# Packs of K and Q by 6 transfers instead of 12, and a first stage that loads only what the first products need

## The reference

```python
# cross-attention, 16 heads of width 16
q = (layernorm(x) @ Wq.T + bq); k = (ctx @ Wk.T + bk); v = (ctx @ Wv.T + bv)
x = x + softmax(q k^T / 4) v @ Wo.T + bo
# feed-forward block: h0 = layernorm(x)
h = h0 + causal_attention_with_rope(rmsnorm(h0, g1), wq, wk, wv) @ wo
y = h + moe(rmsnorm(h, g2), w_router, wg, wu, wd)      # 8 experts, top 2, hidden 704
x = x + y
```

## Time and profile before

| | |
|---|---|
| median of 3 runs | 2783.26 us (2781.7 to 2789.47) |
| the profiled execution's own time | 2782.65 us |
| its span, first to last instruction | 2780.9 us |
| TensorE busy | 2572.7 us, 93% |
| VectorE, ScalarE, GpSimd busy | 64%, 52%, 27% |
| mean granted TensorE clock | 0.958 of full speed |

### The profile page before, as it was taken

How to read it: one execution, slowest core, us unless ns; L and a number is a source line. 1 busy time by engine, 2 the same in 40 slices (tenths; PEclk the granted TensorE clock), 3 DMA queues, 4 the chain that set the end, 5 groups by cost and what they waited for, 6 DMA issues and landing times. The chain is left out here.

```text
span 2780.9 us, 47221 instructions
## 1 busy us (share of the span) xinstructions
PE 2572.7 (93%) x14174; PEld 1302.3 (47%) x14175; DVE 1784.8 (64%) x3812; ACT 1453.5 (52%) x2957; POOL 737.5 (27%) x1327
## 2 busy tenths in 40 slices
PE   7998999999999999999997878999884899999996
PEld 5665233333333333333332543444364677777775
DVE  4665888888888888888882766777455222222221
ACT  2433377777777777777775655677521122222221
POOL 4444000000000000000002664666444333333332
PEclk9999699999999999999998998999886999999998
DMA  6877855455555554445513867987574121212123
GB/s 194 255 232 202 94 62 63 57 61 62 67 68 67 68 60 60 60 59 65 67 20 107 241 200 145 160 162 161 146 225 127 25 34 30 33 31 32 32 32 79
DMA packets 494486, 274.38 MB, mean 99 GB/s; under 512 B 309296, under 2 KB 462784, under 8 KB 494112
## 3 DMA queue, kind: packets, MB, share of 16 engines
q1 hardware_dynamic: 472224, 239.77, 45.0%
q0 software_dynamic: 16192, 30.16, 5.6%
q10 hardware_dynamic: 5888, 2.24, 0.4%
HBM read 172.15 MB, written 103.31 MB: 99 GB/s over the span
## 5 line engine op out<-in xcount | busy, mean ns | idle before, releaser
L892 DVE TENSOR_REDUCE att_cross_neg_max<-att_cross_ps_s 128x1 f32<-128x401 f32 x2048 | 1027.3, 567 | 149.3 <-PE att_cross_ps_s L811 147.0
L986 ACT ACTIVATE att_cross_probs<-att_cross_ps_st 128x512 f32<-128x512 f32 (+1 forms) x1664 | 879.4, 601 | 288.9 <-PE att_cross_ps_st L830 276.7
L811 PE MATMUL att_cross_ps_s<-att_cross_k_pack,att_cross_q_pack 96*128 96x401 bf16 x2048 | 655.8, 343 | 10.5 <-DVEq L878 10.1
L830 PE MATMUL att_cross_ps_st<-att_cross_q_pack,att_cross_k_pack 99*128 99x512 bf16 (+1 forms) x1664 | 630.4, 382 | 6.5 <-ACT att_cross_probs L986 5.0
L845 PE MATMUL att_cross_ps_o<-att_cross_probs,att_cross_v_tiles 128*32 128x512 f32 (+1 forms) x3328 | 443.0, 605 | 0.1
L811 PEld LDWEIGHTS att_cross_ps_s<-att_cross_k_pack,att_cross_q_pack 96*128 96x128 bf16 x2048 | 201.1, 98 | 370.9 <-DVE att_cross_neg_max L892 242.9
L934 POOL CAST att_cross_neg_max_parts<-att_cross_neg_max_merged 128x16 bf16<-128x16 f32 x32 | 6.3, 196 | 1134.7 <-DVE att_cross_neg_max_merged L885 1134.7
L830 PEld LDWEIGHTS att_cross_ps_st<-att_cross_q_pack,att_cross_k_pack 99*128 99x128 bf16 (+1 forms) x1664 | 163.8, 99 | 303.5 <-ACT att_cross_probs L986 192.0
L892 DVE TENSOR_REDUCE att_self_neg_max<-att_self_ps_s 128x1 f32<-128x128 f32 (+3 forms) x512 | 223.0, 485 | 91.9 <-PE att_self_ps_s L814 88.9
L2059 DVE COPY moe_hiddenT<-moe_ps_h 128x256 f32<-128x256 f32 x142 | 60.2, 424 | 296.9 <-PE moe_ps_h L1962 296.9
L986 ACT ACTIVATE att_self_probs<-att_self_ps_st 128x256 f32<-128x256 f32 (+3 forms) x512 | 201.9, 437 | 92.9 <-PE att_self_ps_st L830 84.9
(11 more groups left out here) (220 smaller groups left out, 2881.9 us busy)
## 6 DMA issues: line engine op xcount, KB each, us to landing
att_cross_k_pack<-k_parts SPq DMA_DIRECT2D x192, 200.1 KB, 7.2
k_parts<-in_part SPq DMA_DIRECT2D x72, 256.0 KB, 3.6
in_rows<-in_ctx_dram SPq DMA_DIRECT2D x24, 512.0 KB, 4.6
v_rows<-in_v_biased SPq DMA_DIRECT2D x24, 512.0 KB, 3.7
att_cross_q_pack<-q_parts SPq DMA_DIRECT2D x192, 64.0 KB, 7.9
att_cross_v_tiles<-v_rows SPq DMA_DIRECT2D x128, 96.0 KB
att_self_k_pack<-k_parts SPq DMA_DIRECT2D x192, 64.0 KB, 3.4
att_self_q_pack<-q_parts SPq DMA_DIRECT2D x192, 64.0 KB, 3.4
```

The lines of the kernel that those rows point to most:

```text
L811: mm = nc.tensor.matmul(ps_s[bank][:, 0:w], qp[v.buf][0:SROWS, j, q * P:(q + 1) * P], kp[v.buf][0:SROWS, j, s:s + w], start=True, stop=not ...
L830: mm = nc.tensor.matmul(ps_st[bank_of_step[s]][0:rows, q0:SEQ], kp[u.buf][0:MROWS, j, t * P:t * P + rows], qp[u.buf][0:MROWS, j, q0:SEQ], ...
L892: nc.vector.tensor_reduce(nmax[v.odd][:, j * QT + q, i:i + 1], ps_s[bank][:, 0:w], AX.X, ALU.max, negate=True).then_inc(s_read, 1)
L986: nc.scalar.activation(pr[0:rows, (u.odd * STEPS + s) % RING, q0:SEQ], ps_st[bank_of_step[s]][0:rows, q0:SEQ], ACT.Exp).then_inc(exp_done, 1)
```

## The change

The middle parts of two edits are shown. First, the packs. `q_parts` now holds the parts in the opposite order (slot 0 the low part), so that the parts of K and of Q that stand side by side in a pack are consecutive in DRAM, and one transfer brings 3, 2 or 1 of them. Second, `prepare_weights` loads only the identity, the four weights and three biases, and SP issues the first row's five input loads right behind them. Everything else is loaded by ScalarE's queue at steps 0 to 4 of the last pair of `project_inputs`, and brought into order by ScalarE at steps 6 to 8.

```diff
-K_PARTS = (0, 1, 2, 0, 1, 0)
-Q_PARTS = (0, 0, 0, 1, 1, 2)
-PAIRS = len(K_PARTS)
+RUNS = ((0, 0, 3), (0, 1, 2), (0, 2, 1))
+PAIRS = sum(n for _, _, n in RUNS)
...
     def load_kq(self, eng, v):
-        for r in range(PAIRS):
-            eng.dma_start(self.kp[v.buf][r * HD:(r + 1) * HD, :, :],
-                         self.k_parts[v.batch, K_PARTS[r], :, :].rearrange("(d h) n -> d h n", d=HD)[:, v.heads, :],
-                         max_dma_last_dim=self.kv * 2).then_inc(self.kq_in[v.buf], 16)
-            eng.dma_start(self.qp[v.buf][r * HD:(r + 1) * HD, :, :],
...
+        row = 0
+        for k, q, n in RUNS:
+            for pack, parts, first, length in ((self.kp, self.k_parts, k, self.kv), (self.qp, self.q_parts, q, SEQ)):
+                src = parts[v.batch, first:first + n, :, :].rearrange("a (d h) n -> (a d) h n", d=HD)
+                eng.dma_start(pack[v.buf][row * HD:(row + n) * HD, :, :], src[:, v.heads, :],
+                             max_dma_last_dim=length * 2).then_inc(self.kq_in[v.buf], 16)
+            row += n
...
     # prepare_weights, SP
-                sp.dma_start(keep["constants"][:, :], w["constants"]).then_inc(consts_in, 16)
-                for n in ("Wq", "Wk", "Wv", "Wo"):
-                    sp.dma_start(raw[n][:, :, :], w[n].rearrange("(c p) i -> p c i", p=P)).then_inc(raw_in, 16)
+                sp.dma_start(keep["ident"][:, :], w["constants"][:, 0:P]).then_inc(ident_in, 16)
+                for n in order:                                   # Wk, Wv, Wq, Wo
+                    sp.dma_start(raw[n][:, :, :], w[n].rearrange("(c p) i -> p c i", p=P)).then_inc(raw_in[n], 16)
+                for item in range(inputs.items):
+                    inputs.load(sp, item, 0)
...
     # prepare_weights, ScalarE: 14 transfers and two reorderings become
+                for n in ("bk", "bq"):
...
+                act.dma_start(keep["bv"][:, :], w["bv"].partition_broadcast(P)).then_inc(small_in, 16)
+                act.wait_ge(small_in, 16 * 5)
...
+class LaterWeights:
+    def at_step(self, act, c):
+        if c == 0:
+            self.load(act, keep["constants"][:, P:], w["constants"][:, P:])
+        if c == 1:
+            for n in ("wq", "wk"):
...
+        if c == 6:
+            act.wait_ge(self.came, 16 * self.LOADS)
+            self.reorder("wq").then_inc(self.kept, 1)
+        if c == 7:
+            self.reorder("wk").then_inc(self.kept, 1)
+        if c == 8:
+            for n in ("mask_q", "before"):
...
```

More of the change, by code:

```diff
@@ L227, in with_next, with project_inputs @@
         body((batches - 1, c), (batches - 1, c + ahead) if c + ahead < N else None)
-def project_inputs(nc, ctx_in, x_in, k_parts, v_rows, q_parts, keep, batches, packs):
-    chunks = [(o, min(SEQ, CTX - o)) for o in range(0, CTX, SEQ)]
+def project_inputs(nc, w, inputs, k_parts, v_rows, q_parts, keep, batches, packs):
+    chunks = inputs.chunks
     CHUNKS = len(chunks)
-    ITEMS = CHUNKS + 1
+    ITEMS = inputs.items
     N = 2 * ITEMS
@@ L261, in project_inputs @@
         p = Prog(nc, stack, "in_")
-        rows = [p.sb(f"rows{i}", [P, QT, DIM]) for i in range(ITEMS)]
+        rows, rows_in = inputs.rows, inputs.rows_in
+        later_weights = LaterWeights(nc, p, w, keep)
         normed = p.sb("x_normed", [P, QT, DIM])
@@ L306, in load @@
                 def load(st):
-                    source, length = (x_in, SEQ) if st.tokens else (ctx_in, CTX)
-                    src = source[bass.ds(st.row * length + st.start, st.size), :]
-                    if st.size >= P:
-                        sp.dma_start(rows[st.item][:, 0:st.size // P, :], src.rearrange("(t p) d -> p t d", p=P))\
-                          .then_inc(rows_in[st.item], 16)
-                    else:
-                        sp.dma_start(rows[st.item][0:st.size, 0, :], src).then_inc(rows_in[st.item], 16)
+                    inputs.load(sp, st.item, st.row)
                 def step(st, later):
@@ L344, in step_and_packs @@
                             packs.load_kq(sp, Unit(0, 0))
-                for c in range(ITEMS):
-                    load(Step((0, c)))
                 steps(sp, step_and_packs, ahead=ITEMS)
@@ L470, in step, with step_and_later_weights @@
                            .then_inc(std_ready, 1)
-                steps(act, step)
+                def step_and_later_weights(st, later):
+                    step(st, later)
+                    if isinstance(st.pair, int):
+                        later_weights.at_step(act, st.c)
+                steps(act, step_and_later_weights)
             @block.gpsimd
@@ L488, in _ @@
                 steps(pool, step)
+        p.sems += inputs.p.sems
         p.clear()
```

122 lines of the change are left out of this document (75 added, 47 removed).

## The result

The changed kernel takes 2767.01 us (median of five runs, 2764.15 to 2770.03), the kernel before 2783.26 in the same comparison: a ratio of 0.9935, with a 95% interval from 0.9924 to 0.9947. The sign was right; the time lies 9 us above the range.

What follows compares the result with a forecast made beforehand. TensorE was taken as the bound in most of the projections and cross-attention, leaving three places to gain: 13.4 + 1.5 + 4.6 + 2.2 + 21 - 0.5 = 42.2, so 2782.65 to 2740.5 us; 8-in-10 range 2731 to 2758.

Steps and rivals of the forecast that it cites:

- the three places: Where the change could gain: the first 23.5 us, the 22.2 us from 259.3 to 281.5, and self-attention.
- The start, 13.4: Kernel start: TensorE's first input transposes come at 10.1 instead of 23.54 us, a gain of 13.4 us.
- GpSimd's fills: First row: GpSimd's 18.2 us of memsets and settings make its first cast 4 us late, at no cost; uncovered, 4.
- The clock at the start, 1.5: First input transposes: TensorE, already turning weights, runs them at a higher clock; gain 1.5 us, ends 0 and 1.6.
- The tail, 4.6 and 2.2: End of projections: packs at 180 GB/s instead of 119 shorten the V-store wait by 4.6 us; kept clock gives 2.2.
- The later weights, -0.5 with an end of 4: Last pair of projection rows: loading about 2.3 MB there costs 0.5 us, at most 4.
- Nothing for cross-attention: Cross-attention, 325 to 1450 us: TensorE is busy to within 1.2 us, so fewer transfers there are worth nothing.
- Self-attention, 21: Self-attention: the 23.2 us of pack waits are covered, less a tenth for ScalarE, late next; gain 21 us.
- wait in self-attention is replaced: Self-attention: ScalarE's exponential holds TensorE instead, keeping back half of the 21 us; 2751 us, chance 14 in 100.
- the slower rival: Packs: larger transfers split over fewer DMA engines, 12.7 us a unit against 9.7; 2868 us, chance 3 in 100.

Runs made afterwards that it cites:

- the six edits: Changed kernel plus partition runs 32, 48, 16; later turn in self-attention; four V buffers; SyncE waiting for maxima rows; late weights at fifth item; bv first: 2737.78 us.
- the six edits with the fills moved: The six edits, plus GpSimd's constant fills of packs and V tiles moved into the last pair of rows: 2736.59 us, ratio 0.9834.
- the turn later: Changed kernel with TensorE turning a unit's row maxima at the sixth piece instead of the fourth in self-attention: 2753.48 us.

## Why the prediction was wrong

By its own steps:

- *What bounds the kernel, and where.* Right: the three places were the ones that moved. Wrong was "Nothing that other engines or transfers gain there moves the end". A stage that is busy now can still lose time to what the change makes late in it: self-attention apart, each gain met a wait in a stage that I had passed over as busy (3.1, 4.6 and 4.2 us below).
- *The start, 13.4.* Measured 10.5. That ScalarE "ends sooner" failed: it waited for bv until 11.72. Wo came at 8.9, not 6.7: I took the landing time of a small transfer alone for one among 1 MB of weights, with 1.5 MB of rows behind them. The first chunk, reckoned at 8.4 and hidden, landed at 12.40 and had 0.4 us to spare. With ScalarE out of the way only 0.5 came back (0.8 on the mean of several traces), so the other 2 or so are Wo's landing and the hand-overs behind it. Among the twelve profiled executions with the new start the first transposes come at 12.2 to 14.0.
- *GpSimd's fills, "cost nothing; without that cover 4".* This step failed, 3.1 us. TensorE indeed never waits for a low part. But SP, one list in order, does, and the V store stands behind; V had two buffers and no slack. Moving the fills took the waits away, and so did two more V buffers, all but 0.7 us.
- *The clock at the start, 1.5.* Measured -0.5: the 16 transposes took 3.65 us, as before, and the K product behind them 4.40 against 3.90. What failed is "now it turns weights", taken for a clock that is up by then. The weights' transposes follow each other 0.21 us apart, like the 16 of the rows, and those of the next item 0.11 apart: TensorE was at the lower level all the while. The full clock came at 18.02, in the middle of that K product, whose matmuls first start 0.90 and 0.76 us apart and from then on 0.43. The row of 13.0 to 18.4 us reads 1.00 all the same, because the trace has no record of the clock before 18.02 and a window without a record is counted as full. In one of the twelve executions (the six edits with the fills moved) the first record is at 10.05, and the same 16 took 1.94 us behind 1.9 us of idle; in the others it is at 15.5 to 19.1, and they took 3.3 to 3.7, among them three behind the same 1.9. In the six edits without the moved fills TensorE turned the same weights from 6.09 us on, against 5.98, and its clock rose only at 17.31. So the gain exists, and this work ahead of it does not secure it; why the clock rose early in that one execution stays open.
- *The tail, 4.6 and 2.2.* Measured 2.9 and 0.5. The mechanism was right and the rate off: 158 GB/s, not 180. At 158 the 1.62 MB take 10.3 us, 3.3 less than at 119, which is near what the wait lost. It was still long enough for a slow product of 5.29 us. With the reordered runs, or four buffers, the wait is 1.2 or 0.6 us and the product 3.67: the condition that I named for the 2.2 was right. In all traces no such product is slow behind a wait of up to 1.72 us; behind 1.9 to 2.4 us it comes at either level (5.37 us after 1.90, 3.70 after 2.36).
- *The later weights, -0.5 with an end of 4.* Measured -4.6, beyond that end. "A store of V behind the constants" was named and given too little: 2.8 us of wait and 1.6 in a product at the lower clock, which I had not reckoned with here.
- *Nothing for cross-attention.* Failed by 4.2 us at its first unit. I took TensorE's being busy from 325 us on as cover for everything, but the prologue up to 320.8 is not in that window. SP, freed early by faster packs, sent more of them ahead of 12 KB on which TensorE waits. One wait in SP, or faster packs, removed it.
- *Self-attention, 21.* Measured 15.2. "What is late next is ScalarE": it was GpSimd's split of the maxima, seen before as 2.7 us in 6 waits that the pack waits had hidden. With the turn later the stage gave 28.6 us in all, more than my upper end, 23.2, since that end was the sum of the waits that I saw, not of those behind them.

The terms add up: 10.5 - 0.5 - 3.1 - 4.6 + 3.4 - 4.2 - 0.6 + 0.8 (`project_self`) + 15.2 - 1.1 (behind) = 15.8, against 15.6 by the spans. (What lies behind self-attention takes 779.9 to 783.6 us in the fourteen traces, so the 1.1 is no effect of the change that can be told.) Against the forecast the largest terms that are missing are self-attention (5.8), the first unit of cross-attention (4.2), the later weights (4.1), the tail with its clock (3.4), GpSimd's fills (3.1), the start (2.9) and its clock (2.0). The rival "wait in self-attention is replaced" was the true one in kind, with another engine and about half its price; the slower rival did not occur. And the error of the range was to treat six waits as apart: where a stage is freed, what comes next was priced for one place only.

By the rule of the Trainium skill (SBUF — State Buffer, "Door 1: The DMA port swizzle"), bandwidth goes by how many of 16 ports a transfer's partitions reach. Taken transfer by transfer, it makes the six packs cost as much as 4 of 16 partitions instead of 6; an estimate from it and the measured 119 is 119 times 6/4, or 178 GB/s, and the trace has 158. For the other order its table gives 3 (partitions 0 to 31 load 8 ports equally, 32 to 79 load 12, and 80 to 95 load 4, each with 4 partitions); the estimate is 119 times 6/3, or 238, where the trace has 186 to 194. The ratio of the two orders is 4 to 3 by this estimate, and 1.18 to 1.23 in the traces. The rule picks the right one of two orders with equal bytes, and promises more than either gives.

## What to carry to other kernels

When a wait is to go, look for the next releaser of the same instruction, in waits that are now small because the big one hides them (2.7 us became 14.6). An in-order queue turns a late helper engine into a late store of something else: list what stands behind each wait of the issuing engine, and give the double-buffered tile behind it more buffers first. A queue that is freed early can put its bulk ahead of another queue's small urgent transfer. And read a clock from the pitch of equal instructions as well: a window without a record reads 1.00.

## What the runs showed of the hardware that I had not expected

- Six transfers over 96 partitions, in runs of 48, 32 and 16, go at 158 GB/s; in runs of 32, 48 and 16, at 186 to 194; twelve of 16 partitions at 119. The one transfer that changes much is K's of 48 partitions: 4.31 us from partition 0, 2.19 from partition 32.
- A transfer of 12 KB, on ScalarE's queue, that went through in at most 2.4 us with no packs ahead of it let TensorE wait until 9.7 us after its issue when packs of another queue were ahead.
- The same 16 transposes, behind the same 1.9 us of idle, took 1.94 us in one execution and 3.65, 3.65 and 3.29 in three others. The clock's first record, at full, is at 10.05 us in the first and at 17.82, 17.31 and 16.17 in the others, with the same transposes of weights ahead in all.
